# Memory attention of a two-layer macaron model: rotation by a lane shuffle and products on GpSimd, two layer norms folded into one, scores moved in a segment's step

## The chip, the cores and the metric

The kernel runs on one core of one Trainium2 chip. The metric is the device time of one execution in microseconds (us). A core has TensorE (PE; its weight loads are PEld), VectorE (DVE), ScalarE (ACT), GpSimd (POOL) and SyncE (SP), which run their own instruction streams in order and wait for one another by semaphores. TensorE's clock has two levels, 1.2 and 2.4 GHz; the profile gives the granted clock as a share of full speed.

## The reference, cut to what matters

The program runs six sublayers in a row on x, 4 x 1024 x 128 float32. The change touches only the second, the memory attention of layer 0, which is fed with a normalized x and normalizes it again:

```python
x = x + _L0_attn_ref(_layernorm(x, axis=-1), w_qkv, w_out, ln_g, ln_b, mem_beta)

def _reference_tuple_inner(x, w_qkv, w_out, ln_g, ln_b, mem_beta):
    xn = (x - x.mean) / sqrt(x.var + 1e-05) * ln_g + ln_b
    q, k, v = split(xn @ w_qkv)                  # 16 heads of 64
    qr, kr = rope(q, pos), rope(k, pos)          # t * cos + rot * sin, rot: (-t[1], t[0]) in each pair of channels
    def step(carry, inp):                        # 32 segments of 32 positions, in order
        scores = mask(q_s @ k_s.T * SCALE)       # rotated q and k
        sdpa = softmax(scores) @ v_s
        mem_out = (phi(q) @ mem) / (phi(q) @ z + 1e-6)      # phi = elu + 1, unrotated
        out = beta * mem_out + (1 - beta) * sdpa
        prev_v = (phi(k) @ mem) / (phi(k) @ z)
        mem = mem + phi(k).T @ (v_s - prev_v);  z = z + phi(k).sum
    return outs @ w_out
```

## The kernel before

The stage is `memory_attention_stage` (from L1320 on). A tile is one segment of 32 positions for all four batches, 128 rows; there are 32 tiles, and the memory `mem` (with z as column 65, in SBUF) passes from one to the next. `in_tiles` (L1315) writes tile 0 out, loops over tiles 1 to 29, and writes out the last two. Every engine has its own function `tile(w)`, and the order of calls in it is the order of that engine's work; nothing else schedules.

While tile w is answered, tile w + 1 is projected ("front") and tile w + 2 normalized. On TensorE, `fill_q` and `fill_k` put the q and k projections of the next tile, channels in partitions, into the PSUM banks `front_ps[0]` and `[2]`, and a second time with the weights `w_rot`, in which channel pairs are exchanged and one is negated, into banks 1 and 3. ScalarE copies banks 0 and 2 to `raw` (L1536), VectorE multiplies banks 1 and 3 by sin into `turned` (`front_rope`, L1647), GpSimd multiplies `raw` by cos and adds `turned` (`rope`, L1598 and L1601) into `roped`, which `scores` (L1428) reads. ScalarE takes relu and exp of `raw`, VectorE joins them to phi (`front_phi`, L1656).

For the tile itself: `recall_k` (L1437) asks the memory with phi of k, `back_u` on VectorE (L1703 to L1708) makes u = v less the answer, in two halves; `turn_phi` (L1421) transposes phi of k; `recall_q` asks with phi of q and `back_o` (L1716 to L1724) scales the answers; `additions` (L1463) forms the memory's increments, which `back_mem` (L1730) adds; `answers` transposes o (L1473) and adds exps times v (L1479); ScalarE copies the result to `oT` (L1561), `project` (L1486) multiplies by w_out and `back_x` (L1734) adds it to X. `softmax_1` (L1665 to L1672) scales, masks and shifts the scores, ScalarE exponentiates (L1557), `softmax_2` (L1678 to L1688) sums, scales by (1 - beta) over the sum and transposes in blocks.

The normalization is two rounds on VectorE, `norm_1` to `norm_3`: statistics (L1624, L1626), variance and power on GpSimd (`rstd_of`, L1590, L1592), rescaling (L1633), and all of it again on the result (L1640).

The waits that matter: `scores` wait for both rotations (`rope_done` 2), the second additions for the first memory sum (`mem_done` 1), the answers for `softmax_2` (`pT_ready`) and for the second memory sum, GpSimd's product for the whole copy of q or k (`q_copied`, `k_copied`), `recall_k` for `back_x` of the tile before.

Of the kernel before, what the change touches and what calls it, by code (L numbers as in the profile page):

```python
# [1323 lines left out]
def memory_attention_stage(nc, K, io):  # L1324
# [5 lines left out]
    with ExitStack() as ctx:  # L1330
        sb = lambda name, shape, dt=F32: ctx.enter_context(nc.sbuf_tensor(f"m_{name}", shape, dt))
        w_qkv = sb("w_qkv", [P, 3 * INNER])
        w_rot = sb("w_rot", [P, 2 * INNER])
# [6 lines left out]
        stats, mv = sb("stats", [P, 2, 6]), sb("mv", [P, 2, 2])  # L1340
        var, rstd = sb("var", [P, 2]), sb("rstd", [P, 2])
        xn1, xn2 = sb("xn1", [P, D]), sb("xn2", [P, D])
# [17 lines left out]
        s = stage_sems(nc, ctx, "m", "loaded emptied set_up passed ln_stats ln_mv ln_var ln_rstd xn1_ready xn2_ready xnT_full xnT_ready "  # L1360
                                    "q_full k_full v_full scores_full q_copied k_copied v_copied rot_done cos_done "
# [20 lines left out]
        def _(pe):  # L1382
            def fill(bank, weights, column, full):

                for k in range(4):
                    last = nc.tensor.matmul(front_ps[bank][:, k * P:(k + 1) * P], weights[:, column + k * P:column + (k + 1) * P], xnT[:, :],  # L1386
                                            start=(k == 0), stop=True, skip_group_check=True)
                last.then_inc(full, 1)

            def turn_x(f):  # L1390
                pe.wait_ge(s.xn2_ready, f + 1)
                wait(pe, s.v_copied, at(f, 2, -1))
                nc.tensor.transpose(front_ps[0][:, 0:P], xn2[:, :], c.ident[:, :]).then_inc(s.xnT_full, 1)

            def fill_q(f, half):
                if half == 0:
                    pe.wait_ge(s.xnT_ready, f + 1)
                wait(pe, s.phik_copied, at(f, 2, half - 1))
                fill(2 * half, w_qkv, 512 * half, s.q_full)
                wait(pe, s.scores_read, f)  # L1400
                fill(2 * half + 1, w_rot, 512 * half, s.q_full)

            def fill_k(f, half):
                pe.wait_ge(s.q_copied, at(f, 2, half + 1))
                fill(2 * half, w_qkv, INNER + 512 * half, s.k_full)
                pe.wait_ge(s.rot_done, at(f, 4, half + 1))
                fill(2 * half + 1, w_rot, INNER + 512 * half, s.k_full)
# [16 lines left out]
            def scores(f):  # L1424
                wait_alone(pe, s.rope_done, at(f, 2, 2), s.passed)
# [63 lines left out]
            def tile(w):  # L1489
                more = not (isinstance(w, int) and w == TILES - 1)  # L1490
                recall_k(w)
                turn_phi(w, more)
# [16 lines left out]
                if more:  # L1509
                    scores(w + 1)  # L1510
# [3 lines left out]
            pe.wait_ge(s.set_up, 4)  # L1514
# [6 lines left out]
            scores(0)  # L1521
# [4 lines left out]
        def _(act):  # L1526
# [4 lines left out]
            def front(f, k):  # L1531
                full, copied = ((s.q_full, s.q_copied), (s.k_full, s.k_copied))[k]
                wait(act, s.cos_done, at(f, 2, k) - 1)
                for half in range(2):
                    act.wait_ge(full, at(f, 4, 2 * half + 1))
# [28 lines left out]
            def tile(w):  # L1564
                more = not (isinstance(w, int) and w == TILES - 1)
                soft_exp(w)
                copy_phi(w)
# [19 lines left out]
        def _(pool):  # L1587
            def rstd_of(f, m):
                pool.wait_ge(s.ln_mv, at(f, 2, m + 1))
                nc.gpsimd.tensor_tensor(var[:, m:m + 1], mv[:, m, 1:2], c.eps[:, 0:1], ALU.add).then_inc(s.ln_var, 1)  # L1590
                pool.wait_ge(s.ln_var, at(f, 2, m + 1))
                nc.gpsimd.tensor_tensor(rstd[:, m:m + 1], var[:, m:m + 1], c.minus_half[:, 0:1], ALU.pow).then_inc(s.ln_rstd, 1)  # L1592

            def rope(f, k):
# [3 lines left out]
                nc.gpsimd.tensor_tensor(roped[k][:, :, :], raw[k][:, :, :], wide(cos).broadcast_to([P, PAIRS, P]), ALU.mult).then_inc(s.cos_done, 1)  # L1598
                pool.wait_ge(s.cos_done, at(f, 2, k + 1))
                pool.wait_ge(s.rot_done, at(f, 4, 2 * k + 2))  # L1600
                nc.gpsimd.tensor_tensor(roped[k][:, :, :], roped[k][:, :, :], turned[k][:, :, :], ALU.add).then_inc(s.rope_done, 1)  # L1601

            def tile(w):
# [4 lines left out]
                if norm:  # L1608
                    rstd_of(w + 2, 0)
                    rstd_of(w + 2, 1)  # L1610
# [3 lines left out]
            for f in range(2):  # L1614
                rstd_of(f, 0)
                rstd_of(f, 1)
# [5 lines left out]
        def _(dve):  # L1622
            def stats_of(f, m, source):
                nc.vector.bn_stats(stats[:, m, :], source).then_inc(s.ln_stats, 1)  # L1624
                wait_alone(dve, s.ln_stats, at(f, 2, m + 1), s.passed)
                nc.vector.bn_aggr(mv[:, m, :], stats[:, m, :]).then_inc(s.ln_mv, 1)  # L1626

            def norm_1(f):
                stats_of(f, 0, X[:, f, :])
# [7 lines left out]
            def norm_3(f):  # L1637
                dve.wait_ge(s.ln_rstd, at(f, 2, 2))
                wait(dve, s.xnT_full, f)
                nc.vector.tensor_scalar(xn2[:, :], xn1[:, :], mv[:, 1, 0:1], rstd[:, 1:2], ALU.subtract, ALU.mult).then_inc(s.xn2_ready, 1)  # L1640
# [1154 lines left out]
```

## Time and profile before

| | us |
|---|---|
| median of 3 runs | 3008.43 (3007.99 to 3012.46) |
| the profiled execution | 3012.59 |
| its span, first to last instruction | 3010.8 |
| TensorE busy in the span | 2138.8 (71%) |
| VectorE busy | 2026.5 (67%) |
| ScalarE busy | 1398.5 (46%) |
| GpSimd busy | 1198.5 (40%) |
| mean granted clock of TensorE | 0.805 |

The memory attention takes about 345 to 1194 us of the span. A row of a timeline gives start, duration, engine, line, operation, what is written and read, how many instructions were merged, and in brackets the idle time before it and what ended it. A duration includes the time in which a started instruction could not go on. An instruction of TensorE is listed with its pipeline delay, so one group's end may lie behind the next one's start.

### The profile page before, as it was taken

To read this page: it belongs to the slowest core of one execution; us is meant where nothing else is said; L and a number is where in the kernel's file an instruction comes from. 1 tells how busy PE (TensorE), PEld (TensorE's weight loads), DVE (VectorE), ACT (ScalarE), POOL (GpSimd) and SP (SyncE) were. 2 spreads that over 40 slices of the span, in tenths; PEclk is the share of its full clock that TensorE was granted. 3 is DMA by queue.
4 is the path that set the end of the run, shared out by engine and by line. 5 is a ranking of instruction groups with operands and counts; after the bars stand their busy time and mean duration, and the time that the engine had idled before them with its cause. 6 is when DMAs were issued, how large, how long until landed. Compare 5 with 4: busy or idle time off the path is not lost. (4 is left out here: it accounts for less than half of the span.)

```text
span 3010.8 us, 87503 instructions
## 1 busy us (share of the span) xinstructions
PE 2138.8 (71%) x35326; PEld 1718.5 (57%) x35326; DVE 2026.5 (67%) x4856; ACT 1398.5 (46%) x2361; POOL 1198.5 (40%) x945
## 2 busy tenths in 40 slices
PE   3677399998989887567477966646666555647895
PEld 2566277777777776457356965432322233335795
DVE  5777477777777775767663444659999967655343
ACT  1445244444444442435354532229888854435452
POOL 3645355544444543545454641460000121105463
PEclk7789699999999997679778985665566577868897
DMA  4122300000000000022412230000000000021223
GB/s 103 43 88 67 95 3 0 0 0 0 0 0 0 0 0 3 32 72 77 127 54 72 78 95 6 0 0 1 1 0 0 0 1 1 0 61 37 76 77 111
DMA packets 95267, 104.01 MB, mean 35 GB/s; under 512 B 18936, under 2 KB 81000, under 8 KB 94464
## 3 DMA queue, kind: packets, MB, share of 16 engines
q1 hardware_dynamic: 74416, 64.12, 7.7%
q0 software_dynamic: 18176, 37.79, 3.7%
q8 instruction: 91, 1.49, 0.2%
q14 instruction: 72, 0.59, 0.1%
q10 hardware_dynamic: 2512, 0.02, 0.0%
HBM read 60.00 MB, written 46.20 MB: 35 GB/s over the span
## 5 line engine op out<-in xcount | busy, mean ns | idle before, releaser
L2285 DVE CUSTOM_DVE_ANT_0 be_logs<-be_joint,be_logs 128x1024 f32<-128x1024 f32 x256 | 293.3, 1220 | 7.6 <-ACT be_logs L2258 7.6
L2258 ACT ACTIVATE be_logs<-be_joint,b_tiny 128x1024 f32<-128x1024 f32 x256 | 281.2, 1118 | 9.8 <-PE be_joint L2228 3.4
L2488 POOL TENSOR_TENSOR bw_kT<-b_knT,b_head_of 128x768 f32<-128x768 f32 x40 | 58.5, 1494 | 537.2 <-SPq L2311 380.4
L2228 PE MATMUL be_joint<-be_partsT_k,be_partsT_q 64*128 64x512 f32 x512 | 193.8, 761 | 95.1 <-DVE be_sums L2285 91.6
L405 POOL DMA_INDIRECT d_pairs<-s_y_tile,s_x_tiles x156 | 178.8, 1146 | 121.7 <-DVE s_y_tile L1293 94.9
L1598 POOL TENSOR_TENSOR m_roped_q<-m_raw_q,m_cos 128x1024 f32<-128x1024 f32 x32 | 75.9, 2372 | 351.0 <-ACT m_raw_q L1536 351.0
L405 POOL DMA_INDIRECT d_pairs<-g_y_tile,g_x_tiles x156 | 160.0, 1026 | 139.5 <-ACT g_y_tile L828 103.1
L2228 PEld LDWEIGHTS be_joint<-be_partsT_k,be_partsT_q 64*128 64x128 f32 x512 | 71.5, 275 | 216.4 <-DVE be_sums L2285 211.9
L332 POOL DMA_INDIRECT d_rows<-s_xn,s_slot x128 | 129.1, 1008 | 115.8 <-DVE s_slot L323 81.6
L332 POOL DMA_INDIRECT d_rows<-g_xn,g_slot x128 | 131.1, 1024 | 103.0 <-DVE g_slot L323 68.8
L1142 PE MATMUL s_ps_y<-s_down,s_a_tile 128*128 x1248 | 151.6, 275 | 0.0
L1386 PE MATMUL m_front<-m_xnT,m_w_qkv 128*128 128x128 f32 x1024 | 149.1, 289 | 0.8 <-ACT m_xnT L1529 0.5
L1293 DVE TENSOR_SCALAR s_y_tile<-s_ps_y,s_x_tiles 128x128 f32<-128x128 f32 x156 | 47.5, 346 | 148.2 <-PE s_ps_y L1142 104.9
L1142 PEld LDWEIGHTS s_ps_y<-s_down,s_a_tile 128*128 128x128 f32 x1248 | 145.6, 191 | 0.0
L1212 ACT ACTIVATE s_a_tile<-s_ps_h,s_tile_bias 128x256 f32<-128x256 f32 x312 | 122.9, 475 | 32.8 <-PE s_ps_h L1126 32.8
L1386 PE MATMUL m_front<-m_xnT,m_w_rot 128*128 128x128 f32 x1024 | 136.1, 276 | 0.0
L1386 PEld LDWEIGHTS m_front<-m_xnT,m_w_qkv 128*128 128x128 f32 x1024 | 125.0, 192 | 11.2 <-ACT m_xnT L1529 0.8
L1386 PEld LDWEIGHTS m_front<-m_xnT,m_w_rot 128*128 128x128 f32 x1024 | 125.5, 193 | 0.0
L2355 PE MATMUL bw_exp<-ident,bw_expd 128*96 128x128 f32 x256 | 43.0, 324 | 105.0 <-DVE bw_expd L2513 105.0
L721 PE MATMUL g_ps_h<-g_x_hi,g_up_tile 128*128 128x256 f32 x312 | 101.1, 324 | 11.0 <-DVE g_up_tile L937 10.0
L2080 POOL TENSOR_TENSOR bq_rnorm<-bq_sumsq,bq_half_power 128x64 f32<-128x64 f32 x8 | 84.4, 10546 | 56.9 <-DVE bq_sumsq L2114 56.9
L1601 POOL TENSOR_TENSOR m_roped_k<-m_roped_k,m_turned_k 128x1024 f32<-128x1024 f32 x32 | 104.4, 3262 | 4.8 <-POOL m_roped_k L1598 4.6
(464 smaller groups left out, 6518.4 us busy)
## 6 DMA issues: line engine op xcount, KB each, us to landing
g_x_tiles<-d_rows SPq DMA_DIRECT2D x78, 132.0 KB
s_x_tiles<-d_rows SPq DMA_DIRECT2D x78, 132.0 KB
d_rows<-d_rows SPq DMA_DIRECT2D x32, 132.0 KB
g_shared<-d_pairs SPq DMA_DIRECT2D x8, 512.0 KB, 7.2
g_xn<-d_pairs SPq DMA_DIRECT2D x8, 512.0 KB, 7.5
s_up_raw<-L_ffn_We SPq DMA_DIRECT2D x16, 256.0 KB, 5.4
s_down<-L_ffn_We SPq DMA_DIRECT2D x16, 256.0 KB, 5.7
s_up_raw<-d_pairs SPq DMA_DIRECT2D x8, 512.0 KB, 8.3
```

The costliest lines, as they stand in the source:

```text
L332: nc.gpsimd.indirect_dma_start(out=self.rows[:, :], out_offset=bass.IndirectOffsetOnAxis(ap=r.slot[:, j, m * GROUP + t:m * GROUP + t + 1], ...
L405: nc.gpsimd.indirect_dma_start(out=pairs[:, :], out_offset=bass.IndirectOffsetOnAxis(ap=x_tile[i % LOADS_AHEAD][:, h, D:D + 1].bitcast(U32 ...
L721: nc.tensor.matmul(h, up_tile[b][:, 0, m, part, :], x_hi[b][:, 0:SLOT_ROWS], start=(k % 2 == 0), stop=False, skip_group_check=True)
L1142: last = nc.tensor.matmul(y, a_tile[b][:, k, h * P:(h + 1) * P], down[:, bass.ds(experts[i], 1), k * D:(k + 1) * D], start=False, stop=(k ...
L1212: nc.scalar.activation(a_tile[b][:, k, :], ps_h[2 * b + k // 2][:, (k % 2) * SLOT_ROWS:(k % 2 + 1) * SLOT_ROWS], ACT.Silu, bias=tile_bias[ ...
L1386: last = nc.tensor.matmul(front_ps[bank][:, k * P:(k + 1) * P], weights[:, column + k * P:column + (k + 1) * P], xnT[:, :], start=(k == 0) ...
L1598: nc.gpsimd.tensor_tensor(roped[k][:, :, :], raw[k][:, :, :], wide(cos).broadcast_to([P, PAIRS, P]), ALU.mult).then_inc(s.cos_done, 1)
L1601: nc.gpsimd.tensor_tensor(roped[k][:, :, :], roped[k][:, :, :], turned[k][:, :, :], ALU.add).then_inc(s.rope_done, 1)
L2080: nc.gpsimd.tensor_tensor(rnorm[:, :], sumsq[:, :], half_power[:, :], ALU.pow).then_inc(s.rnorm_ready, 1)
L2228: last = nc.tensor.matmul(joint_ps[k % DEPTH][:, a, :], partsT[0][rows, b, i * P:(i + 1) * P], partsT[1][rows, b, half * 512:(half + 1) * ...
L2258: nc.scalar.activation(logs[k % DEPTH][:, :, :], joint_ps[k % DEPTH][:, :, :], ACT.Ln, bias=A.tiny[:, :]).then_inc(s.log_ready, 1)
L2285: nc.vector.tensor_tensor_reduce(out=flat, in0=joint_ps[k % DEPTH][:, :, :].rearrange("p a j -> p (a j)"), in1=flat, scale=1.0, scalar=0.0 ...
```

## The change

Five things change in the stage, and nothing outside it.

- The turned weights `w_rot` and their 16 matmuls a tile are gone. VectorE makes `turned` from `raw` with one STREAM_SHUFFLE for q and one for k (each lane takes its neighbour's value, `lane ^ 1`), GpSimd multiplies it by sin, in place; the sign of the exchange is put into `sin` once, at the start.
- `rope` on GpSimd is three instructions for q and three for k instead of two. The shuffle waits for the whole copy of q (k), the sin product for the shuffle.
- One normalization with variance * (1 + eps) + eps squared in place of two rounds: one GpSimd exchange less, and one SCALAR_TENSOR_TENSOR with the scale as a broadcast second tensor instead of two TENSOR_SCALAR.
- `scores(w)` is no longer the end of the step before but follows `recall_k(w)`, and banks 1 and 3 hold scores only.
- VectorE's order in a tile becomes: u halves, first softmax, o halves, shuffle of q, second softmax, memory sums; on ScalarE the copy of phi of k comes ahead of the exponential.

```diff
@@ tensor
             def fill_q(f, half):
                 if half == 0:
                     pe.wait_ge(s.xnT_ready, f + 1)
                 wait(pe, s.phik_copied, at(f, 2, half - 1))
-                fill(2 * half, w_qkv, 512 * half, s.q_full)
-                wait(pe, s.scores_read, f)
-                fill(2 * half + 1, w_rot, 512 * half, s.q_full)
+                fill(2 * half, 512 * half, s.q_full)
 
             def fill_k(f, half):
                 pe.wait_ge(s.q_copied, at(f, 2, half + 1))
-                fill(2 * half, w_qkv, INNER + 512 * half, s.k_full)
-                pe.wait_ge(s.rot_done, at(f, 4, half + 1))
-                fill(2 * half + 1, w_rot, INNER + 512 * half, s.k_full)
+                fill(2 * half, INNER + 512 * half, s.k_full)
...
             def scores(f):
+                wait(pe, s.scores_read, f)
                 wait_alone(pe, s.rope_done, at(f, 2, 2), s.passed)
@@ gpsimd
             def rope(f, k):
                 copied = (s.q_copied, s.k_copied)[k]
                 pool.wait_ge(copied, at(f, 2, 2))
                 wait(pool, s.scores_full, f)
                 nc.gpsimd.tensor_tensor(roped[k][:, :, :], raw[k][:, :, :], wide(cos).broadcast_to([P, PAIRS, P]), ALU.mult).then_inc(s.cos_done, 1)
+                pool.wait_ge(s.rot_done, at(f, 2, k + 1))
+                nc.gpsimd.tensor_tensor(turned[k][:, :, :], turned[k][:, :, :], wide(sin).broadcast_to([P, PAIRS, P]), ALU.mult).then_inc(s.sin_done, 1)
                 pool.wait_ge(s.cos_done, at(f, 2, k + 1))
-                pool.wait_ge(s.rot_done, at(f, 4, 2 * k + 2))
+                pool.wait_ge(s.sin_done, at(f, 2, k + 1))
@@ vector
             def norm_2(f):
-                dve.wait_ge(s.ln_rstd, at(f, 2, 1))
-                nc.vector.tensor_scalar(xn1[:, :], X[:, f, :], mv[:, 0, 0:1], rstd[:, 0:1], ALU.subtract, ALU.mult).then_inc(s.xn1_ready, 1)
-                wait_alone(dve, s.xn1_ready, f + 1, s.passed)
-                stats_of(f, 1, xn1[:, :])
...
+                nc.vector.scalar_tensor_tensor(out=xn[:, :], in0=X[:, f, :], scalar=mv[:, 0:1], op0=ALU.subtract, in1=rstd[:, :].broadcast_to([P, D]),
+                                               op1=ALU.mult).then_inc(s.xn_ready, 1)
...
             def front_rope(f, k):
 
                 wait(dve, s.rope_done, at(f, 2, k) - 1)
-                for half in range(2):
-                    dve.wait_ge((s.q_full, s.k_full)[k], at(f, 4, 2 * half + 2))
-                    nc.vector.tensor_tensor(turned[k][:, 4 * half:4 * half + 4, :], front_ps[2 * half + 1][:, :].rearrange("p (k t) -> p k t", t=P),
-                                            wide(sin).broadcast_to([P, 4, P]), ALU.mult).then_inc(s.rot_done, 1)
+                wait_alone(dve, (s.q_copied, s.k_copied)[k], at(f, 2, 2), s.passed)
+                nc.vector.stream_shuffle(turned[k][:, :, :].rearrange("p k t -> p (k t)"), raw[k][:, :, :].rearrange("p k t -> p (k t)"),
+                                         [lane ^ 1 for lane in range(32)]).then_inc(s.rot_done, 1)
```

Where the instructions now stand. VectorE in a tile, from the second half of u to the first half of o, before:

```order
L1703 RECIPROCAL m_rden<-m_back 128x8
L1705 TENSOR_TENSOR m_held<-m_back,m_rden 128x512
L1708 TENSOR_TENSOR m_u<-m_v,m_held 128x2x4x64
L1678 TENSOR_REDUCE m_ssum<-m_exps 128x16
L1680 RECIPROCAL m_srec<-m_ssum 128x16
L1682 TENSOR_TENSOR m_srec<-m_srec,m_one_less_beta 128x16
L1684 TENSOR_TENSOR m_exps<-m_exps,m_srec 128x512
L1688 STREAM_TRANSPOSE m_expsT<-m_exps 128x512
L1716 SCALAR_TENSOR_TENSOR m_rden<-m_back,m_over_beta 128x8
```

The second softmax (L1678 to L1688) stands between u and o. The same engine and tile with the change, from the last half of o on:

```order
L1713 TENSOR_TENSOR m_o<-m_back,m_rden 128x2x4x64
L1636 STREAM_SHUFFLE m_turned_q<-m_raw_q 128x1024
L1667 TENSOR_REDUCE m_ssum<-m_exps 128x16
L1669 RECIPROCAL m_srec<-m_ssum 128x16
L1671 TENSOR_TENSOR m_srec<-m_srec,m_one_less_beta 128x16
L1673 TENSOR_TENSOR m_exps<-m_exps,m_srec 128x512
L1677 STREAM_TRANSPOSE m_expsT<-m_exps 128x512
L1719 TENSOR_TENSOR m_mem<-m_mem,m_back 128x4x260
```

It now stands between the shuffle of q and the first memory sum. GpSimd, one tile of the loop with the change:

```order
L1595 TENSOR_TENSOR m_roped_q<-m_raw_q,m_cos 128x1024
L1597 TENSOR_TENSOR m_turned_q<-m_turned_q,m_sin 128x1024
L1600 TENSOR_TENSOR m_roped_q<-m_roped_q,m_turned_q 128x1024
L1586 TENSOR_SCALAR m_var<-m_mv 128x1
L1589 TENSOR_TENSOR m_rstd<-m_var,minus_half 128x1
L1595 TENSOR_TENSOR m_roped_k<-m_raw_k,m_cos 128x1024
L1597 TENSOR_TENSOR m_turned_k<-m_turned_k,m_sin 128x1024
L1600 TENSOR_TENSOR m_roped_k<-m_roped_k,m_turned_k 128x1024
```

The two sin products (L1597) are new there, and one pair of small instructions is gone.

## Rows read from the trace of the kernel before

**Rows 1.** Page, strip of 40 slices: granted TensorE clock in tenths.

```profile
PEclk7789699999999997679778985665566577868897
```

**Rows 2.** Stretch: us, busy PE, PEld, DVE, ACT, POOL, granted clock, DMA share, GB/s.

```profile
371.00:1155.00 784.00, 704.92 (x24252) 615.42 (x24252) 607.63 (x1102) 325.18 (x458) 387.61 (x242) 0.97 0.00 0
```

**Rows 3.** Timeline of one steady tile, TensorE.

```profile
704.26 1.28 PE L1428 MATMUL m_front<-m_roped_k,m_roped_q 64*32 64x32 f32 x128 [1.11 <-POOL m_roped_k L1601]
...
709.60 0.85 PE L1437 MATMUL m_back<-m_mem,m_phi_qT 64*32 64x65 f32 x64 [0.83 <-DVE m_u L1708]
...
710.38 1.16 PE L1386 MATMUL m_front<-m_xnT,m_w_qkv 128*128 128x128 f32 x8
...
711.37 1.06 PE L1386 MATMUL m_front<-m_xnT,m_w_rot 128*128 128x128 f32 x8
...
715.83 0.91 PE L1463 MATMUL m_back<-m_u,m_phi_k 32*64 32x65 f32 x64 [0.63 <-issue]
...
721.47 1.99 PE L1473 MATMUL m_back<-ident,m_o 32*128 32x32 f32 x64
...
724.80 1.98 PE L1413 MATMUL m_front<-m_w_qkv,m_xnT 128*128 128x512 f32 x4
...
729.68 1.28 PE L1428 MATMUL m_front<-m_roped_k,m_roped_q 64*32 64x32 f32 x128 [1.11 <-POOL m_roped_k L1601]
```

**Rows 4.** Timeline of the same tile, VectorE and ScalarE.

```profile
710.94 0.68 DVE L1678 TENSOR_REDUCE m_ssum<-m_exps 128x16 f32<-128x512 f32 x1
...
712.15 0.69 DVE L1684 TENSOR_TENSOR m_exps<-m_exps,m_srec 128x512 f32<-128x512 f32 x1
...
712.97 0.71 DVE L1688 STREAM_TRANSPOSE m_expsT<-m_exps 128x512 f32<-128x512 f32 x1
...
714.35 0.59 ACT L1536 COPY m_raw_q<-m_front 128x512 f32<-128x512 f32 x1 [2.19 <-PE m_front L1386]
...
715.04 0.69 DVE L1724 TENSOR_TENSOR m_o<-m_back,m_rden 128x512 f32<-128x512 f32 x1
...
716.84 1.23 DVE L1730 TENSOR_TENSOR m_mem<-m_mem,m_back 128x1040 f32<-128x1040 f32 x1
```

**Rows 5.** Timeline, GpSimd and VectorE: first tile, then the steady one.

```profile
358.29 2.36 POOL L1601 TENSOR_TENSOR m_roped_q<-m_roped_q,m_turned_q 128x1024 f32<-128x1024 f32 x1
...
359.25 2.48 DVE L1656 SCALAR_TENSOR_TENSOR m_phi_qT<-m_expo,m_relu 128x1024 f32<-128x1024 f32 x1 [2.48 <-ACT m_expo L1541]
...
723.76 2.36 POOL L1598 TENSOR_TENSOR m_roped_k<-m_raw_k,m_cos 128x1024 f32<-128x1024 f32 x1
...
724.23 1.97 DVE L1640 TENSOR_SCALAR m_xn<-m_xn,m_mv,m_rstd 128x128 f32<-128x128 f32 x1
...
726.12 1.21 DVE L1656 SCALAR_TENSOR_TENSOR m_phi_kT<-m_expo,m_relu 128x1024 f32<-128x1024 f32 x1
...
726.28 3.26 POOL L1601 TENSOR_TENSOR m_roped_k<-m_roped_k,m_turned_k 128x1024 f32<-128x1024 f32 x1 [0.16 <-POOL m_roped_k L1598]
```

**Rows 6.** Timeline of the stage's start and end: slow TensorE, norm, first and last scores.

```profile
350.31 2.07 PE L1386 MATMUL m_front<-m_xnT,m_w_qkv 128*128 128x128 f32 x8 [0.55 <-ACT m_xnT L1529]
...
350.62 0.35 DVE L1633 TENSOR_SCALAR m_xn<-X,m_mv,m_rstd 128x128 f32<-128x128 f32 x1 [0.92 <-POOL m_rstd L1592]
...
352.66 0.35 DVE L1640 TENSOR_SCALAR m_xn<-m_xn,m_mv,m_rstd 128x128 f32<-128x128 f32 x1 [0.93 <-POOL m_rstd L1592]
...
367.37 1.54 PE L1428 MATMUL m_front<-m_roped_k,m_roped_q 64*32 64x32 f32 x128 [5.63 <-POOL m_roped_k L1601]
...
1165.36 1.56 PE L1428 MATMUL m_front<-m_roped_k,m_roped_q 64*32 64x32 f32 x128
...
1182.97 3.64 PE L1473 MATMUL m_back<-ident,m_o 32*128 32x32 f32 x64 [1.43 <-DVE m_mem L1730]
```

**Rows 7.** Table by stretches before the first scores (columns as in rows 2).

```profile
364.00:366.00 2.00, 0.00 (x0) 0.00 (x0) 1.02 (x1) 0.00 (x0) 1.98 (x1) 0.64 0.00 0
...
368.00:370.00 2.00, 2.00 (x145) 1.71 (x136) 1.02 (x3) 0.46 (x1) 0.00 (x0) 0.50 0.03 8
```

More of the change, by code:

```diff
@@ L1382, in _, with fill @@
         def _(pe):
-            def fill(bank, weights, column, full):
+            def fill(bank, column, full):
                 for k in range(4):
-                    last = nc.tensor.matmul(front_ps[bank][:, k * P:(k + 1) * P], weights[:, column + k * P:column + (k + 1) * P], xnT[:, :],
+                    last = nc.tensor.matmul(front_ps[bank][:, k * P:(k + 1) * P], w_qkv[:, column + k * P:column + (k + 1) * P], xnT[:, :],
                                             start=(k == 0), stop=True, skip_group_check=True)
@@ L1491, in tile @@
                 recall_k(w)
+                scores(w)
                 turn_phi(w, more)
@@ L1508, in tile @@
                 project(w)
-                if more:
-                    scores(w + 1)
                 if more and not (isinstance(w, int) and w == TILES - 2):
                     turn_x(w + 2)
-            pe.wait_ge(s.set_up, 4)
+            pe.wait_ge(s.set_up, 2)
             turn_x(0)
@@ L1533, in front @@
                 wait(act, s.cos_done, at(f, 2, k) - 1)
+                wait(act, s.rot_done, at(f, 2, k) - 1)
                 for half in range(2):
-                    act.wait_ge(full, at(f, 4, 2 * half + 1))
+                    act.wait_ge(full, at(f, 2, half + 1))
                     nc.scalar.copy(raw[k][:, 4 * half:4 * half + 4, :], front_ps[2 * half][:, :].rearrange("p (k t) -> p k t", t=P)).then_inc(copied, 1)
@@ L1614, in _ @@
             for f in range(2):
-                rstd_of(f, 0)
-                rstd_of(f, 1)
+                rstd_of(f)
+            pool.wait_ge(s.side_step, 5)
             rope(0, 0)
@@ L1750, in tile @@
                 back_mem(w, 1)
-                if norm:
-                    norm_2(w + 2)
                 if more:
@@ L1766, in _ @@
             dve.wait_ge(s.loaded, 16 * (LOADS - 1))
-            pairs = w_qkv[:, 0:2 * INNER].rearrange("p (i two) -> p i two", two=2)
-            turned_w = w_rot[:, :].rearrange("p (i two) -> p i two", two=2)
-            nc.vector.tensor_scalar(turned_w[:, :, 0], pairs[:, :, 1], -1.0, None, ALU.mult).then_inc(s.set_up, 1)
-            nc.vector.tensor_copy(turned_w[:, :, 1], pairs[:, :, 0]).then_inc(s.set_up, 1)
-            dve.wait_ge(s.set_up, 4)
+            by_two = signs[:, :].rearrange("p (i two) -> p i two", two=2)
+            nc.vector.memset(by_two[:, :, 0], -1.0).then_inc(s.side_step, 1)
+            nc.vector.memset(by_two[:, :, 1], 1.0).then_inc(s.side_step, 1)
+            dve.wait_ge(s.side_step, 2)
+            nc.vector.tensor_tensor(signs[:, :], signs[:, :], c.ident[:, :], ALU.mult).then_inc(s.side_step, 1)
+            dve.wait_ge(s.side_step, 3)
+            nc.vector.tensor_reduce(side[:, :], signs[:, :], AX.X, ALU.add).then_inc(s.side_step, 1)
+            dve.wait_ge(s.side_step, 4)
+            nc.vector.tensor_scalar(sin[:, :], sin[:, :], side[:, :], None, ALU.mult).then_inc(s.side_step, 1)
+            dve.wait_ge(s.set_up, 2)
             nc.vector.reciprocal(over_beta[:, :], beta[:, :])
```

52 lines of the change are left out of this document (23 added, 29 removed).

## The prediction

> **What bounds the kernel now.** I read the strip of 40 slices first, to find the stage [rows 1]: the memory attention is slices 6 to 15, where the granted clock stands at 9 tenths. The table by stretches gives its loop: of 784 us TensorE is busy 705, 608 VectorE, 388 GpSimd, granted clock 0.97 [rows 2]. The timeline of one tile then shows what ends last. A tile lasts from one start of the scores to the next: 704.26 to 729.68, 25.42 us [rows 3]. After the scores VectorE works without a break until it has written the second half of o at 715.73 [rows 4]; the first additions start 0.1 us later [rows 3]. From there TensorE runs without a break through fills, answers, v and the projection, then waits 1.11 us for the last sum of the rotation on GpSimd, which ends at 729.54 [rows 3, 5]. So two pieces in series set the tile: VectorE's chain (softmax first, softmax second, memory answers) and TensorE's fills, with GpSimd just behind. Over all tiles, first scores at 367.37 to last at 1165.36, it is 798.0 us for 31 steps, 25.74 each [rows 6].
>
> One thing beside it decides the change: VectorE and GpSimd shut each other out. In the first tile the phi instruction of VectorE (two SBUF inputs, usually 1.21) is asked for at 359.25, while GpSimd's sum runs from 358.29 to 360.65; phi lasts 2.48 and ends at 361.73, 1.08 after GpSimd lets go [rows 5]. In the steady tile the normalization asks at 724.23, is through at 726.20, with GpSimd's product ending at 726.12; phi goes next, and GpSimd's sum, started at 726.28, takes 3.26 instead of 2.36, ending 2.2 after phi does [rows 5]. I read: whoever comes first holds it for the whole instruction, the next asker comes next; after a wait, 1024 columns cost VectorE 1.08 (512: half, 0.54) and GpSimd 2.2.
>
> **The change, part by part.** Times below count from the start of a tile's scores.
>
> *Fills of the turned weights gone.* Four of 0.99 us (711.37 less 710.38) [rows 3] leave TensorE: 4.0 us per tile. They lay on its unbroken stretch, so by themselves they are worth up to 4.0. On VectorE four products of 0.69 go and two shuffles of 1024 columns come. No shuffle is in the trace. Bounds: 0.71, the 512-column transpose [rows 4], below; 2 x 0.71 = 1.42 above; I take 1.24, as phi's 1.21 and the memory sum's 1.23 for 1024 and 1040 columns are [rows 4, 5]. On that engine it saves 0.3 a tile and nothing on the path. The Trainium skill (VectorE: DVE Perf Modes, the perf-mode tier table) gives about 2400 ns for 2048 columns of a shuffle, an estimate of 1.33 for 1024 at one column a cycle; the sum below would not move by it.
>
> *Norms as one.* It removes one round of statistics, one exchange with GpSimd and the instruction that stands locked out for 1.97 us [rows 5]; its successor has two SBUF inputs and will be locked out in the same place. Hidden in VectorE's time either way; only the start of the stage gains, 2 us.
>
> *Two more products on GpSimd.* Per tile it now has six large instructions of 2.36 instead of four [rows 5], 14.2 us, and 0.75 of small ones for one norm. All six lie between the copy of q and the next scores.
>
> *The order.* Scores go behind the recall of the k answers, the second softmax behind the shuffle of q. The tile, with the durations of rows 3 to 5:
> - TensorE: scores 1.2, turn of phi 1.0 (eight transposes, taken like a fill), recall 0.78, fill 0.99, recall 0.78, fill 0.99, so the last q fill starts at 4.8 and its copy ends at 4.8 + 1.2 + 0.59 = 6.6. VectorE has done its u halves by about 2.6, then softmax first and both o: 6.7. First additions and first k fill: 6.9 to 8.7.
> - GpSimd: cos product of q 6.65 to 9.0. VectorE: shuffle 6.7 to 7.95; 1.21 us later (710.94 to 712.15 [rows 4]) it asks for the scaling of the exponentials, which has two SBUF inputs, at 9.1. GpSimd's sin product has started at 9.0 and holds to 11.4. Scaling ends at 11.9, transpose 12.6, first memory sum 13.8. Only then may the second additions start (13.9): **TensorE idles from 8.7 to 13.9, 5.2 us.**
> - k: additions 13.9, fill 14.8, its copy ends 16.5. VectorE's phi of q is at 16.1 to 17.3, so GpSimd's cos product ends at 17.3 + 2.2 = 19.5, sin at 21.9, phi of k asks meanwhile and ends at 21.9 + 1.1 = 23.0, the sum at 25.2. Scores at 25.4.
> - TensorE on its side: memory sum to 16.1, answers 16.2 to 19.5, v fill to 21.3, projection, turn of x, recall of k 1.4: 25.4 as well.
>
> At full clock the tile is thus 25.4, today's 25.42: what TensorE saves comes back as two more GpSimd instructions and the locks.
>
> *The clock.* Today TensorE idles 1 us here and there. Where it idled 5.63 us, before the scores at 367.37 [rows 6], the granted clock went to 0.64 and was at 0.50 (its level of 1.2 GHz) after the scores had begun [rows 7]. The new idle stretch of 5.2 us, in every tile, is of that kind. At that level a fill took 2.07 against 1.16, plus 0.9 [rows 3, 6], and the turning of o 3.64 against 1.99, plus 1.65 [rows 3, 6]. For the additions I have no such row; between 0 and 0.9, I take 0.4. Additions and k fill lie on both chains: plus 1.3, 26.7. If the turning of o is slow too, 25.4 + 1.3 + 1.65 = 28.4 on TensorE's chain. I take the piece between: **27.4** (slow for additions, fill and a part of the rest), ends 26.7 and 28.4.
>
> *Start and end.* Before the first scores: about 2 earlier by the round of the norm (from the rescaling at 350.62 to that at 352.66 [rows 6]), about 1 by the missing fills, then two more products of 2.36 and about 0.8 of further lock on GpSimd: 2.5 later. Last tile: scores to additions loses the u halves and the second softmax ahead of o (3.2 and 2.7), and 1.3 comes back before the memory sum: 4.6 less.
>
> Sum: 31 x 27.4 = 849.4 against 798.0 is plus 51.4; plus 2.5, less 4.6: plus 49.3. The profiled execution took 3012.6 (span 3010.8); the median of three is 3008.4. So 3057.7, say **3058**.
>
> **Rivals.** A measurement of this kernel tells about 0.2%, 6 us, from no change.
> - *The clock holds* (0.12, faster). For it: the loop has 0.97 today although TensorE waits in every tile. Against: rows 6, 7. Then 31 x 25.4 = 787.4, less 10.6, less 2.1: 2996. [...]
> - *The scaling gets in first* (0.08, faster). It asks 0.1 us after GpSimd's sin product by my table; a shuffle shorter by 0.15, or a pause between GpSimd's instructions (0.17 today between product and sum), turns it. Then the memory sum is 2.2 earlier, idle time 3.0, and GpSimd bounds the tile: 6.65 + 14.2 + 0.75 + locks 2.8 + pauses 0.5 = 24.9. 31 x 24.9 = 771.9: 2980.
> - *Both in part* (0.08, same): clock lost in some tiles only, period 25.7: 3005.
> - *The shuffle is locked out as well* (0.08, slower still). It reads and writes SBUF; statistics from SBUF under a running GpSimd instruction were not delayed, the 2-port normalization was, so rows speak for either. Each shuffle then waits for a cos product and delays the sin product by 1.1: 2.4 a tile, 29.8 and 3132. The Trainium skill (SBUF — State Buffer, SBUF: two separate sides) names as takers of the shared pair only VectorE instructions with two SBUF inputs or in a 2-port mode; by that rule this rival falls and the sum stays; no row here shows it.
> - Forecast (0.64, slower): port and clock as above, 3035 to 3090.
>
> **The numbers.** 3058 is the likeliest case. The range of 8 in 10 leaves out the early scaling and the locked shuffle: 2990 to 3092. Faster 0.12 + 0.08 = 0.20, same 0.08, slower 0.64 + 0.08 = 0.72.
>
> **What would show it.** In the timeline of a steady tile: the scaling of the exponentials at 2.5 to 2.8 us instead of 0.69, the memory sum behind it, a TensorE gap near 5 us before the second additions, granted clock of the loop 0.75 to 0.85, phi of k above 2 us, GpSimd 17 to 18 busy of 27. Wrong if the scaling lasts 0.69, if the clock stays above 0.95, or if the shuffle takes over 1.5.

## The result and the profile after

The changed kernel takes **3318.66 us** (median of 4 runs, 3311.80 to 3326.41), the kernel before 3009.44 on the same chip: a ratio of 1.1027, 95% interval 1.1001 to 1.1053. The prediction had the direction, not the size: 310 us more where 49 were forecast, and outside the range. The profiled execution took 3317.7 us, its span 3315.6, mean granted clock 0.737 (0.805 before).

From the page of the changed kernel, the strip of the granted clock and the queue of instruction transfers (packets, MB, share of 16 engines; the kernel before has 91 packets there):

```profile
PEclk6788676776777776776796899666555558776898
q8 instruction: 207, 3.39, 0.4%
```

Slices 6 to 15 stood at 9 tenths [rows 1]; the stage now stands at 7 and reaches to slice 17. Its loop by stretches, columns as in [rows 2]:

```profile
375.00:1450.00 1075.00, 757.04 (x23166) 640.00 (x23166) 693.31 (x1002) 321.27 (x457) 487.96 (x243) 0.73 0.01 2
```

TensorE is busy 70% of it where it was 90%. How long a tile takes is read from the 32 additions to X, one a tile (instructions of one line: duration in ns, start of the first and of the last), before and after:

```profile
L1734 DVE TENSOR_TENSOR X<-X,m_back x32: 286/289/289, 394.4 to 1193.5; 128x128 f32 x29, 128x128 f32<-128x128 f32 x3
```

```profile
L1723 DVE TENSOR_TENSOR X<-X,m_back x32: 286/288/290, 402.6 to 1494.6; 128x128 f32 x29, 128x128 f32<-128x128 f32 x3
```

Divided by 31 steps, 25.78 us a tile before and **35.23** after: 293 of the 305 us between the spans, and the first tile ends 8 later. The first scores start at 369.74, 2.4 after those of before.

Two things fill the 9.45 us. The first is the one that was forecast. From the timeline of a step, from its first additions to the recall of the next (727.08), a stretch in which nothing else is lost:

```profile
703.84 0.91 PE L1460 MATMUL m_back<-m_u,m_phi_k 32*64 32x65 f32 x64 [0.18 <-issue]
...
704.47 1.37 DVE L1636 STREAM_SHUFFLE m_turned_q<-m_raw_q 128x1024 f32<-128x1024 f32 x1
704.67 1.16 PE L1386 MATMUL m_front<-m_xnT,m_w_qkv 128*128 128x128 f32 x8
...
706.69 2.35 POOL L1597 TENSOR_TENSOR m_turned_q<-m_turned_q,m_sin 128x1024 f32<-128x1024 f32 x1
706.72 2.35 DVE L1671 TENSOR_TENSOR m_srec<-m_srec,m_one_less_beta 128x16 f32<-128x16 f32 x1
709.11 0.69 DVE L1673 TENSOR_TENSOR m_exps<-m_exps,m_srec 128x512 f32<-128x512 f32 x1
...
710.47 1.20 DVE L1719 TENSOR_TENSOR m_mem<-m_mem,m_back 128x1040 f32<-128x1040 f32 x1
...
711.81 1.29 PE L1460 MATMUL m_back<-m_u,m_phi_k 32*64 32x65 f32 x64 [5.98 <-DVE m_mem L1719]
...
713.03 2.08 PE L1386 MATMUL m_front<-m_xnT,m_w_qkv 128*128 128x128 f32 x8
...
715.04 3.64 PE L1470 MATMUL m_back<-ident,m_o 32*128 32x32 f32 x64
...
718.25 3.37 DVE L1645 SCALAR_TENSOR_TENSOR m_phi_kT<-m_expo,m_relu 128x1024 f32<-128x1024 f32 x1
718.61 2.05 PE L1476 MATMUL m_back<-m_expsT,m_v 32*64 32x32 f32 x128
720.59 3.78 PE L1409 MATMUL m_front<-m_w_qkv,m_xnT 128*128 128x512 f32 x4
...
727.08 1.48 PE L1434 MATMUL m_back<-m_mem,m_phi_kT 64*32 64x65 f32 x128 [0.74 <-DVE X L1723]
```

A product of 16 columns stands 2.35 us behind GpSimd's sin product, the memory sum comes late, TensorE idles 5.98 us. Behind the gap everything is slow: k fill 2.08 (was 1.16), turning o 3.64 (1.99), v fill 3.78 (1.98) [rows 3], and exps times v 2.05, where before it took 1.49:

```profile
723.39 1.49 PE L1479 MATMUL m_back<-m_expsT,m_v 32*64 32x32 f32 x128
```

The same step with the change, in the table by stretches:

```profile
708.00:710.00 2.00, 0.00 (x0) 0.00 (x0) 1.93 (x3) 0.00 (x0) 1.86 (x2) 1.00 0.00 0
...
711.00:712.00 1.00, 0.19 (x12) 0.22 (x19) 0.87 (x2) 0.00 (x0) 1.00 (x1) 0.50 0.00 0
...
720.00:724.00 4.00, 4.00 (x52) 2.03 (x43) 1.62 (x1) 1.60 (x2) 3.68 (x2) 0.50 0.00 0
724.00:726.00 2.00, 2.00 (x17) 1.84 (x16) 0.00 (x0) 0.59 (x1) 0.00 (x0) 0.90 0.00 0
```

In this step the clock falls between 710 and 711, when TensorE has idled since 705.8, and stays at 0.50 (1.2 GHz) to past 724. TensorE was busy without a break from 711.8 on. The gap ahead of the second additions stands in every step of the loop: 4.91 us in about half of them, 5.8 to 6.0 in the others.

The second thing was not foreseen. In about every second step TensorE stands still at the start although nothing it waits for is missing (timeline, the start of the same step):

```profile
688.13 0.21 PE L1434 MATMUL m_back<-m_mem,m_phi_kT 64*32 64x65 f32 x1 [2.22 <-issue]
690.92 2.06 PE L1434 MATMUL m_back<-m_mem,m_phi_kT 64*32 64x65 f32 x127 [2.58 <-issue]
...
694.28 1.54 PE L1425 MATMUL m_front<-m_roped_k,m_roped_q 64*32 64x32 f32 x128 [1.29 <-issue]
...
697.66 1.97 PE L1417 MATMUL m_front<-ident,m_phi_kT 128*128 128x128 f32 x8 [1.84 <-issue]
```

The recall is taken apart after one matmul, and 8 us go in four pieces. In that stretch of the kernel the instruction queue moves data, which it hardly did before. Its transfers from 450 to 1150 us, before and after:

```profile
q8 instruction: 2, 0.03, 0.0%
```

```profile
q8 instruction: 84, 1.38, 0.9%
```

That is four packets of 16 KB a step on the average, but they don't come evenly. From 650 to 682 us there are none, from 682 to 720 nine, then none up to 784. From 608 to 650 it was nine too:

```profile
q8 instruction: 9, 0.15, 1.7%
```

So the loop is fetched in about every second pass, and the 35.23 us are a mean of two kinds of steps: without transfers they take 30.3 to 30.9 us, with them 40 to 42 (starts of additions to X: 614.1, 655.7, 686.0, 726.4, 757.1, 787.8).

### The profile page after: what moved, and what is told of

It reads as the page before. It is cut to its first block and busy times, and to the rows that moved or that the text cites. A ratio compares the mean times of both kernels' runs of the same rounds, so it can differ in the third digit from the quotient of the medians.

```text
span 3315.6 us, 85190 instructions
## 1 busy us (share of the span) xinstructions
PE 2198.1 (66%) x34302; PEld 1748.2 (53%) x34302; DVE 2116.4 (64%) x4763; ACT 1395.6 (42%) x2361; POOL 1309.1 (39%) x945
## 5 line engine op out<-in xcount | busy, mean ns | idle before, releaser
L1460 PE MATMUL m_back<-m_u,m_phi_k 32*64 32x65 f32 x4096 | 70.3, 276 | 195.0 <-DVE m_mem L1719 171.9
L1386 PE MATMUL m_front<-m_xnT,m_w_qkv 128*128 128x128 f32 x1024 | 186.8, 339 | 0.5 <-ACT m_xnT L1524 0.5
L1460 PEld LDWEIGHTS m_back<-m_u,m_phi_k 32*64 32x64 f32 x4096 | 61.6, 168 | 205.2 <-issue 205.1
L1386 PEld LDWEIGHTS m_front<-m_xnT,m_w_qkv 128*128 128x128 f32 x1024 | 158.9, 237 | 13.8 <-issue 2.6
L1549 ACT COPY m_phi_k<-m_front 128x512 f32<-128x512 f32 x64 | 36.1, 588 | 261.8 <-PE m_front L1417 261.8
L1532 ACT COPY m_raw_k<-m_front 128x512 f32<-128x512 f32 x64 | 37.1, 581 | 256.9 <-PE m_front L1386 256.9
L1470 PE MATMUL m_back<-ident,m_o 32*128 32x32 f32 x2048 | 113.3, 390 | 1.4 <-DVE m_mem L1719 1.4
L1409 PE MATMUL m_front<-m_w_qkv,m_xnT 128*128 128x512 f32 x128 | 111.9, 1026 | 2.6 <-ACT m_raw_k L1532 2.6
```

Source lines behind the costliest of these rows:

```text
L1409: nc.tensor.matmul(front_ps[2 * half][:, :], xnT[:, :], w_qkv[:, column:column + 512], start=True, stop=True).then_inc(s.v_full, 1)
L1460: last = nc.tensor.matmul(back_ps[rows[r], b, k * AUG:(k + 1) * AUG], phi_k[seg, h * DH:(h + 1) * DH], u[seg, h, :], start=True, stop=True ...
L1470: nc.tensor.matmul(back_ps[:, b, k * SEG:(k + 1) * SEG], o[seg, k * P:(k + 1) * P], c.ident[seg, seg], start=(k == 0), stop=False, skip_gr ...
```

## Experiments

Each set of four ran on another chip, on which the kernel before took 2997, 2898 and 2895 us, so every result stands beside the kernel before of its own set. Tile lengths come from the additions to X, as above.

### Where the loop's code lies

```diff
+            for _ in range(64):
+                pe.sem_inc(s.passed, 1)
             in_tiles(pe, tile)
```

The other two have 128 and 192 in place of 64.

> The changed kernel with 64 semaphore increments put on TensorE once, ahead of its loop over the tiles: they run one time and move the loop's code by 64 instructions. Theory A (the second cause of the loss is that TensorE's instructions are fetched anew in every pass of the loop, depending on where its loop lies): the queue of instruction transfers, 207 packets in the changed kernel and 91 in the kernel before, and the idle time of TensorE that the profile puts down to issue at the recall of the keys, the scores and the turn of phi (60.7, 26.2 and 33.2 us over the stage) change with the place; at a good place packets near 91, no such idle time, a tile of 30.7 us in place of 35.6 and a total near 3318 - 31 x 4.9 = 3166 us. This place may be a good one or not. Rival B (the order recall, scores, turn of phi makes the gaps, wherever the code lies): packets and gaps as in the changed kernel, 3318 us within 0.5%.

> As the run with 64 increments, with 128. Theory A: packets and issue gaps differ between the places, with 91 packets and 3166 us at a good one. Theory B: no difference, 3318 us.

> As the run with 64 increments, with 192. Theory A: at least one of the three places brings the packets to near 91 and the time to 3166 us or lower. Theory B: all three at 3318 us within 0.5%.

Measured: 3167.38, 3177.91 and 3186.50 us, beside 2997.35 for the kernel before: ratios 1.057, 1.061 and 1.063 (intervals within 0.004 of each). All three have 90 packets, none of them between 450 and 1150 us, and a tile of 30.8 to 30.9 us. The recall no longer waits for issue:

```profile
709.87 1.48 PE L1434 MATMUL m_back<-m_mem,m_phi_kT 64*32 64x65 f32 x128 [0.68 <-DVE X L1725]
```

So 64 instructions that do nothing make the kernel some 4% faster, and rival B falls. The increments aren't free: with 192 of them the first recall stands 29.4 us for issue, some 0.15 each, which is the difference between the three.

To see which place is bad, I put the kernel before there.

```diff
+            for _ in range(96):
+                pe.sem_inc(s.passed, 1)
             pe.wait_ge(s.set_up, 4)
             turn_x(0)
```

> The kernel before with 96 semaphore increments on TensorE ahead of its first wait of the memory attention stage, nothing else. Theory A (a loop that lies in 8 pieces is fetched anew in every pass, whatever the kernel): here the loop lies in 8, so the packets rise from 91 to 150 or more, TensorE idles at the start of a tile for issue, and the time is 3075 to 3190 us. Rival (only the changed kernel's order suffers from it): packets 91, time within 0.5% of before.

Measured: 3045.94 us beside 2897.95, ratio 1.0498 (1.0475 to 1.0521). A tile takes 30.9 us. There are 98 packets between 450 and 1150 us, and the pattern of the changed kernel: in about every second step TensorE stands still at the recall (timeline, TensorE):

```profile
661.30 0.47 PE L1437 MATMUL m_back<-m_mem,m_phi_kT 64*32 64x65 f32 x16 [4.74 <-issue]
664.06 1.85 PE L1437 MATMUL m_back<-m_mem,m_phi_kT 64*32 64x65 f32 x112 [2.29 <-issue]
```

148 us for a kernel whose every operation is unchanged. Of six places tried on two kernels, the two where the loop touches 8 pieces of 256 instructions are fetched anew, in about every second pass, and the four with 7 are not. The Trainium skill (Runtime: NRT & Kernel Launch, Instruction fetch mechanics) describes TensorE's instruction memory as a FIFO of 128 KiB filled in blocks of 16 KiB, with a fetch when the target of a taken branch isn't in the current window of two blocks. The packets of 16 KB agree with the block, and the stall at the head of the loop with the branch. The window doesn't agree: with two blocks a loop of 7 would be fetched in every pass too, and at the four places with 7 the queue moves at most 2 packets from 450 to 1150 us. There the measurement decides. Why an eighth piece should matter is not shown, only that the fetching goes with it at these six places.

### The lock, and where the second softmax stands

```diff
                 softmax_1(w)
+                softmax_2(w)
                 back_o(w, 0)
                 back_o(w, 1)
                 if more:
                     front_rope(w + 1, 0)
-                softmax_2(w)
```

> The changed kernel with VectorE's second part of the softmax (sum, reciprocal, two scalings, transpose) put back ahead of the answers o, so it is done before the sin product of GpSimd; TensorE's code and its place are not touched. Theory (the product on VectorE that waits 2.35 us behind GpSimd's sin product delays the first sum of the memory and so makes TensorE idle 5 to 6 us per tile): that product takes under 0.2 us, the idle time of TensorE ahead of the second additions falls from 169 us over the stage to under 90, but VectorE waits for the exponentials ahead of o by 1 to 1.5 us, so a tile gets 2 to 4 us shorter: 3200 to 3260 us. Rival (the sum of the memory is late for another reason, the work in VectorE's queue as such): the gap stays over 4 us and the time within 0.5% of 3318.

Measured: 3125.53 us beside 2997.35, ratio 1.043 (1.038 to 1.049), better than expected; a tile of 29.50. The product takes 0.17 us, and TensorE's wait for the memory sum ahead of the second additions falls from 163 to 7 us between 375 and 1450. The idle time ahead of the first additions grows in turn, from 22 to 104 us. 171 packets remain: with its place left as it was, this kernel still fetches. Then both together, the reference for it, and two tests of what is left.

```diff
+            for _ in range(64):
+                pe.sem_inc(s.passed, 1)
             pe.wait_ge(s.set_up, 2)
             turn_x(0)
```

The reference has this alone, the next run this and the order above.

> The changed kernel with 64 increments ahead of TensorE's first wait of the stage and nothing else: the reference for the runs that stand on that place. Theory (increments there cost nothing, since TensorE waits then anyway; lock and slow clock make a tile 30.7 us): 31 tiles by 5.0 us more than before, less some 5 us at the ends: 149 us more than the kernel before beside it (ratio 1.049 to 1.053). Rival (they cost some 0.15 us each here too): 159 us more.

Measured: 3058.18 us beside 2895.33, ratio 1.0562 (1.0544 to 1.0580), 163 us more; a tile of 30.85. That is more than either expectation, by 14 and by 4 us. The tile is as expected, and TensorE still idles 41.3 us for the first normalized x ahead of the stage (40.3 in the changed kernel), so they lie in time that was idle anyway. What the rest is wasn't followed up.

> The changed kernel with 64 increments in the same place (so that the loop isn't fetched again; there TensorE waits anyway, so that the increments should cost nothing, where they cost some 10 us per 64 right ahead of the loop) and with VectorE's second part of the softmax ahead of the answers o. Theory (lock and instruction fetch are together the whole loss): a tile of 25.7 to 26.5 us and 3010 us, from 2990 to 3040, so the rotation by a shuffle neither gains nor loses. Rival (the work that the change puts on GpSimd and VectorE costs by itself): a tile over 27.5 us, 3060 us or more.

Measured: 2920.13 us beside 2897.95, ratio 1.0074 (1.0044 to 1.0103), a tile of 26.43, as the theory had it. Moving the code and moving the softmax take back all but some 22 us of the loss. What remains is in the timeline:

```profile
650.78 3.16 POOL L1602 TENSOR_TENSOR m_roped_k<-m_roped_k,m_turned_k 128x1024 f32<-128x1024 f32 x1
...
654.05 1.28 PE L1425 MATMUL m_front<-m_roped_k,m_roped_q 64*32 64x32 f32 x128 [0.29 <-issue]
...
664.20 1.29 PE L1460 MATMUL m_back<-m_u,m_phi_k 32*64 32x65 f32 x64 [4.08 <-issue]
665.42 2.08 PE L1386 MATMUL m_front<-m_xnT,m_w_qkv 128*128 128x128 f32 x8
```

TensorE now idles ahead of the first additions (o comes after the softmax), and the scores start 0.1 us after GpSimd's last sum.

### What the clock costs

The four matmuls read w_qkv twice and write a bank that nobody reads; they add nothing to the result.

```diff
                     fill_k(w + 1, 0)
+                for _ in range(4):
+                    nc.tensor.matmul(front_ps[1][:, :], w_qkv[:, 0:P], w_qkv[:, 0:512], start=True, stop=True, skip_group_check=True)
                 additions(w, 1)
```

> The changed kernel with 64 increments in that place and, between the first k fill and the second additions of each tile, four products of 128x512 on TensorE whose results nobody reads, in the stretch in which it stands idle; VectorE's order as in the changed kernel, lock and all. Theory (the lock costs only the idle stretch, and what makes a tile 30.7 us in place of some 26.5 is the clock of 0.50 after it): the second additions take 0.9 us in place of 1.3, the second k fill 1.2 in place of 2.1, turning o 2.0 in place of 3.6, the v fill 2.0 in place of 3.8; a tile of 26.5 to 27 us and 3033 us, from 3015 to 3050. Rival (the tile is bound by GpSimd or VectorE, the slow clock is hidden behind them): 3130 us or more. Without the extra products this kernel should take 3157 us.

Measured: 2961.89 us beside 2897.95, ratio 1.0214 (1.0194 to 1.0234), 64 us more; a tile of 27.69. The rival is out, and the theory had hoped for more: 26.5 to 27 us a tile.

```profile
651.45 3.60 PE L1501 MATMUL m_front<-m_w_qkv 128*128 128x512 f32 x8
...
656.53 0.91 PE L1460 MATMUL m_back<-m_u,m_phi_k 32*64 32x65 f32 x64 [1.49 <-DVE m_mem L1723]
...
657.37 1.16 PE L1386 MATMUL m_front<-m_xnT,m_w_qkv 128*128 128x128 f32 x8
...
658.86 1.99 PE L1470 MATMUL m_back<-ident,m_o 32*128 32x32 f32 x64 [0.34 <-DVE m_mem L1723]
...
662.39 3.39 PE L1409 MATMUL m_front<-m_w_qkv,m_xnT 128*128 128x512 f32 x4
```

Useless work of 3.6 us in the gap makes each tile 3.2 us shorter. The lock is as it was (VectorE's product 2.10); fill and turning o are fast again, the v fill mostly not: the clock falls to 0.50 at 662, although after the useless work TensorE had idled only twice, for 1.49 and 0.34 us. So of the 5.07 us that a tile without fetching is longer than before, at least 3.2 are the clock.

The same in front of the first additions of the kernel with the early softmax:

```diff
                     fill_q(w + 1, 1)
+                wait(pe, s.scores_read, w + 1)
+                for _ in range(4):
+                    nc.tensor.matmul(front_ps[1][:, :], w_qkv[:, 0:P], w_qkv[:, 0:512], start=True, stop=True, skip_group_check=True)
                 additions(w, 0)
```

> The run with the early softmax, and four products of 128x512 on TensorE ahead of the first additions, where it idles 4.1 us. In that run the first additions take 1.29 us, the k fill 2.08 and the second additions 1.30, at a clock of 0.50. Theory (there GpSimd's chain sets the tile: from the shuffle of q to the sum of k it is busy without a gap, and the scores follow 0.1 us behind it): these take 0.9, 1.2 and 0.9 us, and the time stays: 15 to 25 us more than before, as the run without them. Rival (the clock sets the tile): 1.3 to 1.7 us less per tile, 18 to 30 us less than before.

Measured: 2924.55 us beside 2895.33, ratio 1.0106 (1.0090 to 1.0123), 29 us more where the theory had 15 to 25, a tile of 26.35. Additions 0.91, k fill 1.16, and no time won: there the clock is hidden, and by the rows above it is hidden behind GpSimd.

### The parts alone

The norm, in the kernel before: the change's `rstd_of`, `norm_1` and `norm_2`, without its other parts.

```diff
                 back_mem(w, 1)
-                if norm:
-                    norm_2(w + 2)
...
-                    norm_3(w + 2)
+                    norm_2(w + 2)
@@ gpsimd
-                    rstd_of(w + 2, 0)
-                    rstd_of(w + 2, 1)
+                    rstd_of(w + 2)
```

> The kernel before with the two layer norms as one and nothing else of the change. As the prediction has it, the norm itself is hidden; but two small operations less on GpSimd and one product of 1.97 us less on VectorE stand ahead of the k part of the rotation, for which TensorE waits 22.3 us over the stage ahead of the scores. Theory: 0 to 1 us less per tile, 2975 to 2997 us where before takes 2997. Rival (nothing on the path): within 0.2% of before.

Measured: 2868.96 us beside 2897.95, ratio **0.9894** (0.9877 to 0.9912), a tile of 24.78. It is the fastest of all, and gained more than the 0 to 22 us of the theory. GpSimd's queue says why, first before, then here:

```profile
721.95 1.21 POOL L1590 TENSOR_TENSOR m_var<-m_mv,eps 128x1 f32<-128x1 f32 x1 [1.27 <-DVE m_mv L1626]
...
723.24 0.55 POOL L1592 TENSOR_TENSOR m_rstd<-m_var,minus_half 128x1 f32<-128x1 f32 x1
```

```profile
697.47 0.55 POOL L1593 TENSOR_TENSOR m_rstd<-m_var,minus_half 128x1 f32<-128x1 f32 x1 [0.16 <-POOL m_var L1590]
698.46 2.85 POOL L1599 TENSOR_TENSOR m_roped_k<-m_raw_k,m_cos 128x1024 f32<-128x1024 f32 x1 [0.44 <-ACT m_raw_k L1536]
```

Before, k was copied at 721.27, but the second round of the norm stood ahead of the cos product in the queue, one operation on a single column locked for 1.21 us (0.19 in the run); the product began at 723.76 [rows 5]. With one norm the product starts as soon as k is copied, and TensorE no longer waits for the rotation.

The scores back at the end of the step before (with them the softmax orders of the kernel before on VectorE and ScalarE):

```diff
 def tile(w):
     recall_k(w)
-    scores(w)
...
     project(w)
+    if more:
+        scores(w + 1)
```

> The changed kernel with 64 increments as in the reference run, but with the scores back at the end of the step before, and VectorE's and ScalarE's softmax in the order of the kernel before: the rotation and the single norm alone. In the run with the early softmax GpSimd's sum of the k part ends 3.4 us after the projection; TensorE would wait for it before it may recall the keys. Theory: a tile of 27 to 28 us, 65 us more than before (from 40 to 75), so that moving the scores is worth having: some 40 us. Rival (where the scores stand makes no difference, since the recall is the next work of the path anyway): within 10 us of the run with the early softmax, that is 12 to 32 us more than before.

Measured: 2958.94 us beside 2895.33, ratio 1.0219 (1.0202 to 1.0236), 64 us more; a tile of 27.71. As the theory had it: against the run with the early softmax, the move and the orders that go with it are worth 1.3 us a tile, some 40 us.

The last one turns VectorE's order so that nothing that can be locked out stands ahead of a memory sum:

```diff
     front_rope(w + 1, 0)
-    softmax_2(w)
     back_mem(w, 0)
+    softmax_2(w)
     norm_1(w + 2)
     back_mem(w, 1)
+    softmax_3(w)
...
 def answers(w):
     pe.wait_ge(s.mem_done, at(w, 2, 2))
-    wait_alone(pe, s.pT_ready, w + 1, s.passed)
...
                          start=(k == 0), stop=False, skip_group_check=True)
+    wait_alone(pe, s.pT_ready, w + 1, s.passed)
```

Here `softmax_2` is only the sum and the reciprocal; `softmax_3` is the product, the scaling and the transpose. On TensorE the wait now stands between turning o and the answers.

> The changed kernel with 64 increments as in the reference run, and: on VectorE the first sum of the memory straight behind the shuffle of q, then sum and reciprocal of the softmax, and product, scaling and transpose only behind the second sum of the memory; on TensorE the wait for the transposed weights between turning o and the answers. What the sin product locks out is then not ahead of the sums of the memory. Theory: second additions without an idle stretch, so that clock stays at 1.0 up to turning o; the answers wait 1 to 2 us for the transpose; GpSimd's chain ends 1.3 us earlier than with the early softmax; a tile of 24.0 to 25.5 us, 37 us less than before (from 55 less to 10 less). Rival (the phi of k, pushed back behind GpSimd's last sum, becomes the bound of the recall): a tile over 26 us, 10 us more than before or worse.

Measured: 2885.09 us beside 2895.33, ratio 0.9969 (0.9956 to 0.9981), a tile of 25.30: 10 us less than before, at the edge of the expected bounds. The wait for the transpose still costs the clock: most tiles take 24.3 to 24.6 us, with the v fill slow and the answers in part, and every third or fourth takes 26.0, in which the projection is slow too:

```profile
707.63 2.05 PE L1476 MATMUL m_back<-m_expsT,m_v 32*64 32x32 f32 x128 [1.71 <-DVE m_expsT L1682]
709.61 3.78 PE L1409 MATMUL m_front<-m_w_qkv,m_xnT 128*128 128x512 f32 x4
713.18 2.30 PE L1483 MATMUL m_back<-m_w_out,m_oT 128*128 128x128 f32 x16
```

No run shows the rotation by a shuffle to pay. The norm is in this kernel too, and alone it gives 29 us; with the rotation and the best order tried, 10 are left. Beside the norm alone on the same chip, the run with the early softmax is 51 us slower (2920.13 against 2868.96).

## Why the prediction was wrong

In tiles: 25.78 before, 27.4 forecast, 35.23 measured. The runs split the 9.45: 4.38 are the fetching (35.23 less 30.85), 136 us over 31 steps; 5.07 are the rest, 157 us, of which at least 98 are the clock (3.16 a tile). Of the 5.07, the early softmax takes back 4.42 (30.85 less 26.43), lock, gap and slow clock together, and leaves 0.65. The two causes don't simply add: with the early softmax fetching costs 3.07 a tile (29.50 less 26.43).

- *Fills gone, and paid back.* Right. The second additions were put 13.9 us after the start of the scores at full clock; without fetching they start 14.2 after (711.15 to 725.37 in the run with 64 increments).
- *Shuffle taken at 1.24.* It takes 1.35 to 1.37, within the bounds, with GpSimd's cos product running beside it: it isn't locked out, and that rival falls. The Trainium skill's rule (SBUF — State Buffer, SBUF: two separate sides) agrees with the row, and so does the estimate of 1.33 from the Trainium skill's figure (VectorE: DVE Perf Modes, the perf-mode tier table).
- *The scaling locked out behind the sin product.* The mechanism is right, the instruction was the one ahead of it: the product of 16 columns asks 0.03 us after GpSimd has begun, and waits as long as a large one would (2.35; median of all tiles 2.11). The scaling (L1673) takes 0.69, which the prediction had named as a sign of being wrong. It was locked out in one tile, in which the small product took 0.17. I had listed only the large instructions with two SBUF inputs.
- *TensorE idles 5.2 us.* 4.9 to 6.0 in every tile of the loop. Right.
- *The clock: plus 2.0 a tile.* This step failed in size. I let the slow stretch cover additions, a k fill and part of turning o. It covers all of turning o, exps times v and the v fill too. The rows, slow less fast: additions 0.38, k fill 0.92, turning o 1.65, exps times v 0.56, v fill 1.80, together 5.3 where I had put 2.0; and 25.4 plus 5.3 is 30.7, the length of a tile without fetching (30.85), outside the ends of 26.7 and 28.4. The ends weren't ends: I had bounded each slow instruction and not how many there would be, and the row with 3.64 for turning o [rows 6] already showed one that late after an idle stretch. GpSimd, which I had level with TensorE, ends before it in this tile.
- *Missing from the sum: fetching.* The sum put it at nothing without a reason, no rival had it, and with 4.38 us a tile it is nearly as large as lock and clock together. The rows of before show no such transfer in the loop; that they can begin when code moves could have been asked, since the change alters the length of TensorE's code ahead of the loop, by 384 instructions.
- *Norm as one: hidden.* Wrong for the kernel before. It is hidden in VectorE's time; in GpSimd's queue it stood ahead of the cos product of k. Alone it is worth 29 us; what it is worth within the changed kernel no run separates. I had walked its instructions on one engine and not on the other.
- *Start 2.5 later, last tile 4.6 less.* The first scores are 2.4 later, right. From the last scores to the last addition to X it was 28.1 us and is 25.8: 2.4 less, not 4.6.
- *What would show it*: memory sum late, gap near 5, phi of k above 2 (3.37) were seen; the clock of the loop (0.73) fell below the 0.75 to 0.85 given. Without fetching it is 0.78, and GpSimd is busy 16.1 us of a tile of 30.85, not 17 to 18 of 27. The direction doesn't rest on the fetching: without it the kernel is still 163 us slower than before, which is over three times the 49 forecast.

The rivals in which the clock holds or the scaling gets in first did not come about. The run with matmuls in the gap shows that even a clock that mostly holds leaves the kernel 2% slower than before, not faster, as that rival had it. A shorter gap doesn't save the clock either: in the run with the early softmax TensorE stands idle from 660.1 to 664.2, and from 662 on the granted clock is 0.5.

What stays open: how the 4.4 us of fetching a tile divide into standing still and the slow clock that follows it, why the loop is fetched only in some of the passes, and why with the early softmax these are fewer (every second to fourth step, 171 packets) than with the changed order (nearly every second, 207), for the same code in the same place. No run was made that separates them.

## What to carry to other kernels

Before blaming or crediting a change of order in a loop of some 1500 instructions on one engine, look at the instruction queue in the loop and run the same kernel with some idle instructions ahead of it; the place of the code was worth 4 to 5% here. When an operation is moved next to another engine's long SBUF instruction, list every instruction behind it, the 16-column ones too, and for every operation removed walk the queues of all engines that it passed through. And where a new idle stretch is of a size that already lowered the clock somewhere in the trace, price everything that follows it at the low level, as far as the rows show it staying low; here that was some 13.5 us.
